# Eigen-graph layer kernel: tridiagonalization moved first, graph layers and LSTM moved under the leaf QL sweeps

## What is computed

```python
x = layernorm(x + gnn0(x, adj))      # two graph layers, then LSTMs over windows of nodes
x = layernorm(x + gnn1(x, adj))      # spectral layer

# gnn0
h = relu(einsum('ts,bsh->bth', adj, x @ Wg0 + bg0))
h = relu(einsum('ts,bsh->bth', adj, h @ Wg1 + bg1))
for p in 1..4:                        # windows of p nodes; LSTM number p runs over them
    last = lstm_last(..., windows of p nodes of h)
    h[:, every p-th node] = last
# gnn1
deg = ...; L_norm = D^-1/2 (diag(deg) - adj) D^-1/2
_, U = eigh(L_norm)                   # 512 x 512, needs adj alone
h = relu((U^T x) @ W1 + b1); out = U (h @ W2 + b2)
```

## Time and profile before

| | |
|---|---|
| runs of the kernel | 6138.32, 6142.67, 6146.78 us (median 6142.67) |
| profiled execution, device time | 6142.25 us |
| its span (first to last instruction) | 6140.3 us |
| DVE busy | 4298.1 us, 70% |
| PE busy | 3288.7 us, 54% |
| ACT busy | 931.5 us, 15% |
| POOL busy | 787.0 us, 13% |

### The profile page before, as it was taken

One profiled execution on the slowest core, in us unless ns is written; L12 is line 12 of the kernel. 1 busy time (PEld: TensorE's weight loads), 2 busy tenths in 40 slices (PEclk: granted clock), 3 DMA queues, 4 the chain that ended last, 5 costly groups with the idle time before them and its releaser, 6 DMA issues.

```text
span 6140.3 us, 78861 instructions
## 1 busy us (share of the span) xinstructions
PE 3288.7 (54%) x19000; PEld 2346.4 (38%) x19000; DVE 4298.1 (70%) x27212; ACT 931.5 (15%) x4314; POOL 787.0 (13%) x3424
## 2 busy tenths in 40 slices
PE   7877828888888888777777730000002212230476
PEld 4333226566566666666666630000002212120243
DVE  1222286666677777888888889999968888889534
ACT  2432201111122222222222210000000000000000
POOL 0000001111111111111100014444430000000000
PEclk9988855555555555555555555555555555565578
DMA  2000000000000000000000000000000000000000
GB/s 55 0 0 0 0 0 1 1 1 1 1 1 1 1 1 1 1 1 1 1 1 1 1 1 1 1 1 1 1 1 0 0 0 0 0 0 0 0 0 27
DMA packets 20805, 17.38 MB, mean 3 GB/s; under 512 B 6544, under 2 KB 16784, under 8 KB 20368
## 3 DMA queue, kind: packets, MB, share of 16 engines
q1 hardware_dynamic: 20368, 12.65, 0.8%
HBM read 8.41 MB, written 4.20 MB: 2 GB/s over the span
## 4 chain that ended last, share of the span: by engine, by line
DVE 53%; PE 37%; issue 6%; ACT 2%; SPq 1%; POOL 0%; DVEq 0%; DMA 0%; ACTq 0%; POOLq 0%
PE bank L492 9%; PE bank L441 5%; PE bank L504 5%; PE bank L496 3%; PE bank L443 2%; DVE qp L1198 2%; PE bank L475 2%; DVE ycol L939 2%; DVE dif L1551 2%; PE bank L487 2%; DVE ts L971 1%; DVE qp L1188 1%; DVE tau_row L955 1%; DVE jcol L963 1%; DVE gated L953 1%
## 5 line engine op out<-in xcount | busy, mean ns | idle before, releaser
L492 PE MATMUL bank<-lapw,hid 128*32 128x160 f32 (+3 forms) x10200 | 660.4, 421 | 59.5 <-DVE lapw L912 16.2
L529 PE MATMUL bank<-diag,blk 128*128 128x32 f32 (+1 forms) x96 | 23.3, 416 | 1038.9 <-DVE diag L1315 1027.4
L492 PEld LDWEIGHTS bank<-lapw,hid 128*32 128x32 f32 x10200 | 394.8, 162 | 184.8 <-DVE lapw L974 83.0
L504 PE MATMUL bank<-xp,ones 128*128 128x1 f32 x1020 | 298.9, 362 | 277.9 <-DVE xp L963 277.9
L529 PEld LDWEIGHTS bank<-diag,blk 128*128 128x128 f32 x96 | 21.4, 328 | 1040.9 <-DVE diag L1315 1029.4
L441 PE MATMUL bank<-hid,onehot 128*128 x504 | 337.2, 789 | 120.1 <-DVE ga L741 67.2
L502 PE MATMUL bank<-xp,ones 128*128 128x1 f32 x1020 | 299.0, 362 | 185.3 <-DVE xp L945 185.3
L224 POOL TENSOR_TENSOR sq<-hid,ltm 128x4 f32<-128x4 f32 (+3 forms) x510 | 100.7, 198 | 2309.9 <-DVE hid L966 2251.2
L504 PEld LDWEIGHTS bank<-xp,ones 128*128 128x128 f32 x1020 | 255.3, 311 | 321.5 <-DVE xp L963 321.5
L502 PEld LDWEIGHTS bank<-xp,ones 128*128 128x128 f32 x1020 | 255.4, 311 | 229.0 <-DVE xp L945 229.0
L475 PE MATMUL bank<-xn,ones 128*128 128x2 f32 x1020 | 299.3, 363 | 18.5 <-DVE xn L892 17.6
(11 more groups left out here) (729 smaller groups left out, 8474.9 us busy)
## 6 DMA issues: line engine op xcount, KB each, us to landing
out_x<-xs SPq DMA_DIRECT2D x16, 256.0 KB, 3.2
lapw<-in_adj SPq DMA_DIRECT2D x1, 1024.0 KB, 5.8
bias_rows<-in_L_gnn_bg SPq DMA_DIRECT2D x8, 64.0 KB, 5.7
hid<-lz SPq DMA_DIRECT2D x32, 1.0 KB, 1.7
bias_rows<-in_L_gnn_b SPq DMA_DIRECT2D x4, 64.0 KB, 6.0
wg<-in_L_gnn_Wg SPq DMA_DIRECT2D x2, 64.0 KB, 11.1
wg<-in_L_gnn_W SPq DMA_DIRECT2D x2, 64.0 KB, 3.6
xs<-in_x SPq DMA_DIRECT2D x1, 0.5 KB, 19.6
```

Of the source, the lines that this page charges most:

```text
L492: m = pe.matmul(bank[1][32 * q:32 * q + 32, 0:(T + 1) * 32].rearrange("p (u i) -> p u i", i=32), acols[:, t, k:k + 1].to_broadcast([P, 32] ...
L504: pe.matmul(bank[2][:, 4 * NB:4 * NB + 1], ones[:, 0:P], xp[:, 1:2], start=True, stop=True).then_inc(vp_ps, 1)
```

## The change

- DVE's queue begins with the Laplacian's preparation. `x` is loaded last in SP's queue. PE first transposes `adj`, makes the degrees, then transposes the LSTM weights (which still wait for the DMAs of all weights), then enters the tridiagonalization.
- The graph layers and the LSTM have no work on DVE any more. Their PE part stands after the tridiagonalization. A list `WINDOWS` cuts the ACT part into 32 windows; window w is put in ACT's queue between the second and third root of sweep w. Windows 0 to 8 are graph layers, 9 to 31 hold the 36 LSTM steps, one or two in each. A window with LSTM steps ends with a dummy square root.
- Biases bg0 and bg1 are added on PE: for each product of 128 columns one more matmul with a single row of ones.
- Cell and state products of the LSTM run on POOL. In its queue, window w + 1 stands before the rotations of sweep w.
- The sweep body is rewritten: the squares of the off-diagonal are carried instead of formed, one reciprocal in the head is gone; what needs the third root (the rotations' cosines and sines) is moved from the tail into iterations 0 to 7 of the next sweep (`rotation_block`), and the root itself is of 40 columns instead of 60.
- After the sweeps DVE adds the transposed hidden state to `xs` and does the first layer norm in place, with operations of 128 x 2048 in place of those of 128 x 512 and 128 x 128. POOL clears `vt` (`memset`, 128 x 2048) after the 16 back-transposes, and only then can the leaf blocks be copied.

```diff
@@ windows
+    out = [["xt0", "y0"]]
+    for g in range(GROUPS):
+        out.append([f"h1{g}"] + ([f"xt{g + 1}"] if g + 1 < GROUPS else []) + [f"z{g}"])
+        out.append([f"h2{g}"] + ([f"y{g + 1}"] if g + 1 < GROUPS else []))
+    todo = list(range(len(STEPS_L)))
+    while todo:
+        now = [todo.pop(0)]
+        if todo and STEPS_L[todo[0]][2] == 0:
+            now.append(todo.pop(0))
+        out.append(now)
@@ SyncE
             sp.dma_start(lap, adj.rearrange("(t p) n -> p t n", p=P)).then_inc(s_in, 16)
-            sp.dma_start(xs[:], x.rearrange("b (t p) d -> p b t d", p=P)).then_inc(s_x, 16)
...
+            sp.dma_start(xs[:], x.rearrange("b (t p) d -> p b t d", p=P)).then_inc(s_x, 16)
@@ GpSimd
+            def lstm(n):
...
+                for h in range(2):
+                    g = gact[h]
+                    pool.wait_ge(gates_sb, 2 * n + h + 1)
+                    if t == 0:
+                        pool.tensor_tensor(cell[:, h, cs], g[:, 0, cs], g[:, 2, cs], ALU.mult).then_inc(cell_ready, 1)
+                    else:
+                        pool.tensor_tensor(part[:, h, cs], g[:, 0, cs], g[:, 2, cs], ALU.mult).then_inc(lstm_link, 1)
+                        pool.tensor_tensor(part2[:, h, cs], g[:, 1, cs], cell[:, h, cs], ALU.mult).then_inc(lstm_link, 1)
+                        parts[0] += 2
+                        pool.wait_ge(lstm_link, parts[0])
+                        pool.tensor_tensor(cell[:, h, cs], part[:, h, cs], part2[:, h, cs], ALU.add).then_inc(cell_ready, 1)
+                for h in range(2):
+                    g = gact[h]
+                    pool.wait_ge(tanh_ready, 2 * n + h + 1)
+                    if t < p - 1:
+                        pool.tensor_tensor(state[:, h, cs], g[:, 3, cs], g[:, 2, cs], ALU.mult).then_inc(state_ready, 1)
...
             for w in range(SWEEPS):
                 h = w % 2
+                if w + 1 < len(WINDOWS):
+                    window(w + 1)
                 pool.wait_ge(rot_ready, w + 2)
...
+            pool.wait_ge(back_ps, B)
+            pool.memset(vt, 0.0).then_inc(vt_clear, 1)
@@ ScalarE
             for w in range(SWEEPS):
                 act.wait_ge(root_in, 3 * w + 1)
                 act.activation(lq[:, 14:16], lq[:, 12:14], ACT.Sqrt).then_inc(root_out, 1)
                 act.wait_ge(root_in, 3 * w + 2)
                 act.activation(bh[:, 1:2], bh[:, 0:1], ACT.Sqrt).then_inc(root_out, 1)
+                if w < len(WINDOWS):
+                    window(w)
+                if w < len(WINDOWS) and isinstance(WINDOWS[w][-1], int):
+                    act.activation(warm[:, 1:2], warm[:, 0:1], ACT.Sqrt)
                 act.wait_ge(root_in, 3 * w + 3)
-                act.activation(qr[:], qp[:, 0:60], ACT.Sqrt).then_inc(root_out, 1)
+                act.activation(qr[:], qs[:], ACT.Sqrt).then_inc(root_out, 1)
@@ TensorE
+            def biased(into, rows_, i, weights):
+                for t in range(NT):
+                    ts = slice(t * D, (t + 1) * D)
+                    pe.matmul(into[:, ts], ones[0:1, 0:P], bias_rows[0:1, i, ts], start=True, stop=False)
+                    m = pe.matmul(into[:, ts], rows_[:, t * P:(t + 1) * P], weights, start=False, stop=True)
@@ VectorE
+            def rotation_block(n, w):
+                h = w % 2
+                if n == 0:
+                    dve.wait_ge(rot_used, w + 1)
+                    mark(V.memset(rot[:, h, 0, :], 1.0))
+                    mark(V.memset(rot[:, h, 1, :], 0.0))
+                    mark(V.tensor_scalar(qh[:, 0:40], qs[:], 0.5, None, ALU.mult))
+                if n == 1:
+                    dve.wait_ge(root_out, 3 * w + 3)
+                    mark(V.reciprocal(qt[:], qr[:]))
...
+                if n == 7:
+                    V.tensor_scalar(rot[:, h, 2, :], rot[:, h, 1, :], -1.0, None, ALU.mult).then_inc(rot_ready, 1)
...
                     pair_block(M - 1 - i, w)
+                    if w:
+                        rotation_block(M - 1 - i, w - 1)
...
+            for g in range(GROUPS):
+                m = V.tensor_reduce(stat[:, 0, 16 * g:16 * g + 16], nodes(g), AX.X, ALU.add)
...
+            for g in range(GROUPS):
+                m = V.tensor_tensor(nodes(g), nodes(g), across(1, g), ALU.subtract)
...
+                m = V.tensor_tensor(squares[g], nodes(g), nodes(g), ALU.mult)
...
+                m = V.tensor_reduce(stat[:, 2, 16 * g:16 * g + 16], squares[g], AX.X, ALU.add)
...
+                V.tensor_tensor(nodes(g), nodes(g), across(3, g), ALU.mult).then_inc(x1_done, 1)
```

More of the change, by code:

```diff
@@ L65, with lstm_steps, inputs_ready, windows @@
 PRODS, ASKS = job_counts()
+def lstm_steps():
+    return [(p, i, t) for p in range(1, 5) for i in range(lstm_shape(p)[3]) for t in range(p)]
+STEPS_L = lstm_steps()
+STEP_AT = {key: n for n, key in enumerate(STEPS_L)}
+def inputs_ready(p, i):
+    if p == 1:
+        return 0
+    last = (i + 1) * 2 * lstm_shape(p)[0] // (2 * lstm_shape(p - 1)[0]) - 1
+    return 2 * (STEP_AT[p - 1, last, p - 2] + 1)
+def windows():
+    out = [["xt0", "y0"]]
[8 more added lines that the diff above has]
+        out.append(now)
+    return out
+WINDOWS = windows()
 def program(nc, x, adj, wg0, bg0, wg1, bg1, wih, whh, bih, bhh, w1, b1, w2, b2, out):
@@ L385, in _ @@
             pe.wait_ge(s_const, 4)
+            for t in range(NT):
+                pe.matmul(bank[0][:], ones[:, 0:P], lap[:, t, :], start=(t == 0), stop=(t == NT - 1))
+            for t in range(NT):
+                for u in range(NT):
+                    m = pe.transpose(bank[4 + t][:, u * P:(u + 1) * P], lap[:, u, t * P:(t + 1) * P], ident[:])
+                m.then_inc(adj_ps, 1)
+            pe.wait_ge(pre_ops, 1)
+            for t in range(NT):
+                m = pe.matmul(bank[1][:, t * P:(t + 1) * P], ones[:, 0:P], wide[:, t, :], start=True, stop=True)
+            m.then_inc(pre_prods, 1)
             pe.wait_ge(s_w, 16 * 21)
+            pe.wait_ge(adj_sb, NT)
             for i in range(2):
@@ L448, in _ @@
-            with pe.Fori(0, GROUPS) as i:
-                for j in range(NT):
-                    pe.wait_ge(back_in, 4 * i + (j + 1))
-                    for t in range(NT):
-                        m = pe.transpose(bank[j][:, t * P:(t + 1) * P], ga[:, j, t * P:(t + 1) * P], ident[:])
-                    m.then_inc(back_ps, 1)
-                pe.wait_ge(back_used, 4 * i + 4)
-            for t in range(NT):
-                pe.matmul(bank[0][:], ones[:, 0:P], lap[:, t, :], start=(t == 0), stop=(t == NT - 1))
@@ L457, in _ @@
-            pe.wait_ge(pre_ops, 1)
-            for t in range(NT):
-                m = pe.matmul(bank[1][:, t * P:(t + 1) * P], ones[:, 0:P], wide[:, t, :], start=True, stop=True)
-            m.then_inc(pre_prods, 1)
+            pe.wait_ge(wt_sb, 8)
             pe.wait_ge(pre_ops, 2)
@@ L518, in _ @@
+            pe.wait_ge(back_used, B)
             for lv, n in enumerate(LEVELS):
@@ L1217, in _ @@
+                since(c)
+                c = mark(V.copy_predicated(e2, two, la[:, 15, 0:M]))
                 since(b)
[L1218 to L1224 removed]
@@ L1249, in _ @@
+            link(V.reciprocal(stat[:, 3, :], stat[:, 3, :]))
+            for g in range(GROUPS):
+                V.tensor_tensor(nodes(g), nodes(g), across(3, g), ALU.mult).then_inc(x1_done, 1)
+            dve.wait_ge(x1_done, GROUPS)
             dve.wait_ge(vt_in, 16 * (LB + 1))
```

468 lines of the change are left out of this document (243 added, 225 removed).

## The result

The changed kernel takes 5595.38 us (median of four runs, 5594.4 to 5597.63) against 6143.55 us (6138.32 to 6146.78): a ratio of 0.9109, with a 95% interval of 0.9093 to 0.9125. The profiled execution took 5595.16 us, of which the span is 5593.4. The forecast was 5490 us, the range 5335 to 5660. So direction and range held, and the forecast was 105 us too low.

The account below looks back on a forecast made before the run. Stages run in series, with DVE bounding the sweeps while PE and ACT carry the first block. 6142.3 - 844.3 + 0.8 - 11 + 177 + 5 + 20 = 5490 us, range 5335 to 5660.

Parts of the forecast that it names:

- Front: Start of the kernel: first Householder column at about 53.4 us instead of 897.7, -844.3 us.
- The risk named there: Kernel start: PE must transpose LSTM weights before answering the second request; late weights slip the column 0 to +10 us.
- Tridiagonalization and its clock: Tridiagonalization keeps its instructions and 2706.3 us, with the granted clock again at 0.50 (1.2 GHz).
- Sweep body: Each sweep: tail -1.45, head -0.3, operations moved into iterations +1.45 us; net -0.3 per sweep, -11 us for 36.
- POOL's operations: LSTM windows: 216 POOL operations on SBUF stop DVE, losing 0.95 us per long and 0.6 per short one, +177 us.
- Rival (a): LSTM windows: POOL doesn't stop DVE for two-input operations; POOL becomes the bound; about 5350 us, chance 0.16.
- (c): LSTM windows: the POOL product is dear, 2.4 us; about 5710 us, chance 0.09.
- Windows: ACT and PE work placed under the sweeps fits, barely for graph layers; +5 us for all windows.
- the latter doubled by the bias rows: Graph windows on PE: two weight products at 3.67 us, doubled for bias, within 44 us per group against 49 us.
- rival (d): Sweeps: ACT isn't back for the first root and DVE waits out the windows; about 5810 us, chance 0.05.
- rival (b): Graph windows: PE stays at 1.2 GHz under the sweeps, a group costs 88 us; about 5645 us, chance 0.08.
- End of sweeps: Between last sweep and next stage: DVE's additions and layer norm passes take 59 us instead of 39, +20 us.

Follow-up runs that it names:

- experiment 9: Changed kernel with the load of x back right behind the adjacency in SP's queue, ahead of the small weights: 5595.47 us, first Householder column at 61.5 instead of 54.2 us.
- experiment 4: Changed kernel with the LSTM's 216 products and sums on POOL replaced by empty instructions: 5405.27 us, sweeps 9 to 31 568.9 us.
- experiment 5: Changed kernel without 14 of the 15 rotations per sweep on POOL, LSTM products kept: 5568.15 us, sweeps 9 to 31 739.3 us.
- Experiment 7: Changed kernel with POOL's 216 LSTM operations replaced by constant fills of the same tiles: 5403.53 us, sweeps 9 to 31 572.6 us.
- experiment 8: Changed kernel with POOL's 216 LSTM operations each reading one tile instead of two (times a constant): 5475.18 us, sweeps 9 to 31 647.3 us.
- experiment 1: Changed kernel with the one-row bias products of the graph layers left out: 5511.6 us, sweeps 1 to 8 198.5 us.
- experiment 3: Changed kernel with narrow bias products given a 128-row stationary operand (ones in row 0, zeros below): 5506.2 us, sweeps 1 to 8 199.0 us.

## Why the prediction came out as it did

**Front, right.** 54.2 us for 53.4. The risk named there (0 to +10 us if the weights still came at 39.4) was put at 0 since `x` had moved; experiment 9 moved it back and got 7.3.

**Tridiagonalization and its clock, right**: 0.50 again, 2740.1 us for 2739.2.

**Sweep body, a small miss.** 24.85 us for 24.64: the gain was 0.1 us per sweep, not 0.3.

**POOL's operations, right in number, wrong in part in the reason.** The price of the operation (1.27 and 0.91 us forecast; 1.27 to 1.31 and 0.91 to 0.93 measured) and the term (177 for 192.7 us) held; the loss was 1.05 us per long operation in the windows of two steps where I had said 0.95. Rival (a) is out by experiments 4 and 5, (c) by the durations. But I had carried over the earlier trace rows, a write of POOL against a one-input operation of DVE, to two-input operations beside POOL reads. Experiment 7 shows that a write leaves those alone: the row I rested the term on was of another pair. The sentence I had quoted less exactly than it stands, "SBUF — State Buffer" in the Trainium skill, section "SBUF: two separate sides", names the pair: for two SBUF inputs of DVE the lock counts only against a GpSimd operation that reads SBUF. Experiments 7 and 8 agree with it in that, but not in the lock being held for a whole instruction: beside an operation of POOL with one input, DVE's two-input operations were let go after 0.62 of 1.50 us. That the term came out near its measure is in part luck, since it rested on a pair that doesn't occur in the recurrence.

**Windows, wrong: +5 us forecast, +82 measured in sweeps 0 to 8.** The step that failed is "the latter doubled by the bias rows": I took a one-row product at the price of the 128-row product of the earlier trace rows, 0.115 us a record, and its neighbour as unchanged. At that price the biased products of a group are 14.7 us; measured they are 158.6/4 = 39.7 us. Of the 25 us between them 12 come from the switches at full clock (64 pairs at 0.42 us are 26.9 us) and 13 from the fall of the clock. In sweeps 0 to 8 PE is busy 18.2 + 280.2 us, 6.6 of them with the LSTM: 73 us per group instead of 44. Two sweeps of 24.85 don't cover that, and DVE waits for the first root behind it. The waits are what rival (d) describes, in the graph windows alone, and the low clock is what rival (b) describes; but experiments 1 and 3 show both to be results of the one-row operand. I had written that it fits, barely, and then priced the one term on which that hung from a row of another shape, without a bound above it. The LSTM windows fitted as forecast, with no cost beside the products (experiment 4).

**End of sweeps, right**: 61.7 us for 59, POOL and the 20.23 us of block DMAs beneath DVE's passes. By its own price of 2.28 us a pass is 9.1 us and not 8.9, and twelve POOL products at 1.27 us are 15.2 us and not 16.5; neither slip changes the forecast by more than 1 us.

## What to carry to other kernels

Price each operand shape from a row of its own shape; where none exists, bound it on both sides, above all where a cover is called tight. A bias added by a one-row product between full products nearly doubled the price of both here (0.42 for 0.22 us at full clock, 0.72 for 0.43 at half): give it a full stationary operand (one row of ones, zeros below), or one wide product per bank. Before handing elementwise products to POOL beside a busy DVE, compare what DVE loses to it, which is most of POOL's length (here 0.97 to 1.05 of 1.29 us), with what DVE would need itself (0.67 us, of which 0.55 showed in the sweep).

## What the runs showed of the hardware that I had not expected

- A product of 128 columns with a one-row stationary operand, alternating with one of 128 rows, takes 0.42 us a pair of records at full clock and 0.72 at half, and so does its neighbour; with 128 rows in both it is 0.22 and 0.43. The loads last the same (0.50 us a pair at half clock); at a switch they don't overlap the product before. With the one-row operand the granted clock fell in the midst of such a run (0.99 to 0.50), with 128 rows it rose (0.50 to 1.00).
- POOL beside two-input operations of DVE: fills cost DVE 3.7 us in 216, one-input operations of 1.06 to 1.57 us 78, two-input operations of 0.9 to 1.3 us 193. Halving the operations lowers the loss by 22 us though POOL is then busy for longer.
- One-input operations of DVE differ beside POOL's products: L1295, TENSOR_SCALAR of one column, kept its 195 ns (202 at most); L1205, the same of 15 columns, went from 202 to 1154 ns at most; the copy of two columns (L1185) took 691 to 1206 ns instead of 136.
- The small rotations on POOL (operations of 32x32) cost DVE 0.9 us in a sweep of 24.8 without a window.
